# The last stage of an audio tower on one core: GpSimd sums the experts and ends both norms, and every engine gets a new order

## The chip, the cores and the metric

The kernel runs on one core of a Trainium2 chip. The core has five engines with queues of their own: TensorE (matmul, written PE in the profile), VectorE (DVE), ScalarE (ACT), GpSimd (POOL) and SyncE (SP, here the issuer of DMAs). They agree by semaphores. The metric is the device time of one execution in microseconds, and it is compared by medians of several runs.

## The reference, cut to what matters

Five parts run one after the other on 32 batches of 375 tokens with 64 features: token selection, relative attention, experts with top-2 gates, slice attention, and a last part of query experts, the only one touched here. Cut to its steps:

```python
# x: [32, 375, 64]; NH = 4 heads, NE = 4 query experts, d = 16
sx = einsum('bsh,ndh->bnsd', x, hl_w) + hl_b
q, k, v = einsum(sx, wq), einsum(sx, wk), einsum(sx, wv)      # q has NE experts
att = softmax(einsum('bnesd,bntd->bnest', q, k) * d**0.5 + causal)
out = einsum('bnest,bntd->bnesd', att, v); out = where(sx == 0, 0, out)
gs = softmax(einsum(out, gate_w) + gate_b)
mixed = einsum('bnsed,bnse->bnsd', out, gs)                   # sum over the experts
resid = sx[arange(nh), arange(nh)]                            # "the first heads"
hn = layernorm(mixed + resid, ln_g, ln_b)                     # norm 0, over 16 features
hx = where(fx == 0, 0, relu(fx @ fc1.T + b1)); hx = where(fx == 0, 0, hx @ fc2.T + b2)
hx = layernorm(hx + fx, fnorm_g, fnorm_b)                     # norm 1
out = fout * softmax(fout @ fgate_w.T)[..., None]; h = h + out
```

## The kernel before, in words

`query_experts` is a software pipeline over the 32 batches. Every engine has a function `step(r, par)` with the calls of round r in a written order; `bs[i]` is batch r - i, which is i rounds behind the newest one (a lag of i), and `LAGS` is the greatest lag. The helper `rounds` (line 263) writes the first LAGS + 3 rounds out, rounded up so that the rest divides by three, then makes a hardware loop over three rounds a turn, and writes the last LAGS rounds out. With LAGS = 5 that is 8 rounds, 8 turns of the loop and 5 rounds. Nothing but the written orders and the semaphores sets when work happens.

What happens to one batch, with its lag in the kernel before:

- Lag 0: VectorE takes the statistics of the input norm (`start_norm`), GpSimd its root (`take_norm_root`, lines 1253 and 1255), VectorE applies it, and TensorE turns the input and projects queries and keys in three matmuls (`project`, L2201). ScalarE copies each result twice, as bf16 (`first_part`, L2472) and whole (`whole`, L2476). GpSimd then splits it into three bf16 parts: `leave_rest` (L2891) and two instructions of `other_parts` (L2895, L2896), once for each of the three.
- Lag 1: the rest of the splitting, and on SyncE `stack`: it waits for all parts, stores them to DRAM in one DMA (L2157), waits for that, and loads them with 12 DMAs as six stacked groups of rows, into Q (L2161) and K (L2163). TensorE projects the values. `store` writes a finished batch.
- Lag 2: `scores_for_max` in 28 units (L2230, with a mask matmul, L2219), the first of which waits for `stack`. VectorE takes each maximum (L2685).
- Lag 3: `turn_max` on TensorE (L2267), `keep_max` on ScalarE, whose DMA puts the negated maxima into a row of Q. Then `scores_for_exp` in 28 units (L2242, L2219), ScalarE's exponentials (L2495), and `weigh_values` (L2256; e is the expert and jt the column tile, so that 3,2 is the last). ScalarE keeps each expert's context (`keep_context`, L2500), and GpSimd masks it (`mask_context`, L2903).
- Lag 4: the last units of these (exponential scores 24 to 27, values 2,2 and 3,x, context 3 and its mask), `select` and its copies, the gates, and `weigh_experts` (L2659), all on VectorE but for the matmuls and exponentials. Then on VectorE `add_experts` (two instructions of L2663) and `add_first` (one more). Then `centre` and `variance` of norm 0 with the squares on ScalarE, on GpSimd `take_root` (L2911 to L2914: scale, eps, power -1/2, times gamma), on VectorE `finish_mixed` (times the root L2659, plus beta L2663), on TensorE `turn_mixed` (L2285).
- Lag 5: two layers, norm 1 in the same manner (`finish_out` on VectorE), `turn_out` (L2303), the last gate, `hand_out`.

`wait_ge` waits until a semaphore has a value, `own.link` is a wait of an engine for its own instruction. The orders in `step` begin on TensorE with `scores_for_max` 0 and 1, then `turn_max`, `first_layer`, 2, and `weigh_values` 2,2. The last `weigh_values` (3,2) stands behind 9 units for the maximum and 7 for the exponentials. On ScalarE `keep_context` 3 stands behind exponential 3 and `keep_values`.

Of the kernel before, what the change touches and what calls it, by code (L numbers as in the profile page):

```python
# [23 lines left out]
D = 64  # L24
# [2048 lines left out]
def query_experts(k, res, qk_dram, out):  # L2073
# [24 lines left out]
    LAGS = 5  # L2098
    with ExitStack() as ctx:
# [31 lines left out]
        max_stacked = sem("max_stacked")  # L2131
        e_ready, e_done, v_done, c_kept, c_masked = map(sem, ("e", "e_done", "v_done", "c_kept", "c_masked"))
        sel_ready, sel_read, wc_done, g_ready, gex_done, sq_ready, sq_done, vs_ready, root_done = map(
            sem, ("sel", "sel_read", "wc", "g", "gex", "c", "sq", "vs", "root"))
# [13 lines left out]
        def _(sp):  # L2148
# [33 lines left out]
        def _(pe):  # L2182
# [131 lines left out]
            def step(r, par):  # L2314
                on, bs = [alive(r - i, nb) for i in range(LAGS + 1)], [r - i for i in range(LAGS + 1)]
                s = [(par - i) % 3 for i in range(LAGS + 1)]
                if on[2]:
                    scores_for_max(bs[2], s[2], 0)
                    scores_for_max(bs[2], s[2], 1)
                if on[3]:  # L2320
                    turn_max(bs[3], s[3])
                if on[5]:
                    first_layer(bs[5], s[5])
                if on[2]:
                    scores_for_max(bs[2], s[2], 2)
                if on[4]:
                    weigh_values(bs[4], s[4], 2, 2)
                    scores_for_exp(bs[4], s[4], 24)
                    scores_for_exp(bs[4], s[4], 25)
                if on[2]:  # L2330
                    scores_for_max(bs[2], s[2], 3)
                    scores_for_max(bs[2], s[2], 4)
                if on[5]:
                    second_layer(bs[5], s[5])
                if on[2]:
                    scores_for_max(bs[2], s[2], 5)
                if on[4]:
                    scores_for_exp(bs[4], s[4], 26)
                    scores_for_exp(bs[4], s[4], 27)
                    weigh_values(bs[4], s[4], 3, 0)  # L2340
                if on[3]:
                    scores_for_exp(bs[3], s[3], 0)
                if on[1]:
                    project_values(bs[1], s[1])
                if on[2]:
                    scores_for_max(bs[2], s[2], 6)
                if on[4]:
                    weigh_values(bs[4], s[4], 3, 1)
                if on[3]:
                    scores_for_exp(bs[3], s[3], 1)  # L2350
                if on[2]:
                    scores_for_max(bs[2], s[2], 7)
                    scores_for_max(bs[2], s[2], 8)
# [640 lines left out]
```

## Time and profile before

| what | value |
|---|---|
| median of 3 runs | 3435.04 us (3432.09 to 3435.05) |
| profiled execution | 3466.84 us, span 3465.1 us |
| busy, share of the span | PE 90%, DVE 76%, ACT 53%, POOL 37% |
| the last stage | from about 2060 us to the end |
| the costliest line in it | L2685, the maxima on DVE: 896 instructions |

In the profile times are us from the start of the span unless marked ns. A number in brackets behind a row is the idle time of that engine ahead of the instruction, with what ended it. The granted clock (PEclk) is the mean share of TensorE's full speed in that stretch. "issue" is time in which the engine waited for nothing that the profile shows.

### The profile page before, as it was taken

What the parts mean: (1) busy time and instruction counts of PE and PEld (TensorE: products, weight loads), DVE (VectorE), ACT (ScalarE), POOL (GpSimd) and SP (SyncE); (2) the same over time, 40 slices, a digit from 0 to 9 for tenths busy, and PEclk for the clock granted to TensorE, in tenths of its full rate; (3) what the DMA queues carried; (4) which work ended last, traced back from release to release, by engine and by line L of the source; (5) the groups of instructions that cost most, each with busy time, mean ns of one, the idle gap of its engine ahead of it and who ended that gap; (6) DMA issues with size and microseconds to landing.
All of it is one profiled execution on the core that took longest, in us unless ns stands there. A gap on an engine that the chain in (4) does not pass through costs nothing. (4 is left out here: it accounts for less than half of the span.)

```text
span 3465.1 us, 81189 instructions
## 1 busy us (share of the span) xinstructions
PE 3104.9 (90%) x24976; PEld 2206.2 (64%) x24976; DVE 2647.0 (76%) x7766; ACT 1820.8 (53%) x4488; POOL 1289.4 (37%) x1356
## 2 busy tenths in 40 slices
PE   0599999999999799989999956999999999999995
PEld 0488888888888544436777734666666666666663
DVE  4788888888887588866888844788778777877773
ACT  0255555555555455546666612555555555555552
POOL 0344444444444244420000003455445444544432
PEclk9999999999999899997888856899889988988896
DMA  4100000000000000000000005334334333333330
GB/s 136 35 22 16 20 20 14 20 20 14 20 20 2 1 1 0 0 0 1 0 0 0 0 1 80 56 57 71 61 60 66 58 58 58 57 59 67 63 43 4
DMA packets 114142, 111.03 MB, mean 32 GB/s; under 512 B 67960, under 2 KB 105336, under 8 KB 113432
## 3 DMA queue, kind: packets, MB, share of 16 engines
q1 hardware_dynamic: 112792, 106.85, 17.2%
q8 instruction: 137, 2.24, 0.3%
q14 instruction: 189, 1.55, 0.2%
q10 hardware_dynamic: 1024, 0.39, 0.0%
HBM read 76.01 MB, written 30.82 MB: 31 GB/s over the span
## 5 line engine op out<-in xcount | busy, mean ns | idle before, releaser
L2685 DVE TENSOR_REDUCE qe_top<-psum 125x1 f32<-125x375 f32 (+2 forms) x896 | 501.6, 597 | 260.5 <-PE psum L2219 257.1
L2495 ACT ACTIVATE qe_E<-psum 125x375 f32<-125x375 f32 (+1 forms) x896 | 459.7, 531 | 298.7 <-PE psum L2219 281.0
L2219 PE MATMUL psum<-bconst 125*125 125x125 bf16 (+2 forms) x1792 | 494.5, 276 | 0.0
L611 PE MATMUL psum<-Q,K 96*125 96x125 f32 (+3 forms) x2304 | 404.5, 311 | 0.4 <-ACT E L822 0.4
L2230 PE MATMUL psum<-qe_K,qe_Q 96*125 96x375 bf16 (+2 forms) x1536 | 334.5, 301 | 63.1 <-DMA qe_K<-query_key_parts 35.0
L611 PEld LDWEIGHTS psum<-Q,K 96*125 96x125 f32 (+1 forms) x2304 | 334.5, 189 | 24.5 <-issue 1.2
L2242 PE MATMUL psum<-qe_Q,qe_K 97*125 97x375 bf16 (+2 forms) x1536 | 339.7, 301 | 2.4 <-ACT qe_E L2495 2.0
L1161 POOL TENSOR_TENSOR Q<-rot 64x375 f32<-64x375 f32 (+1 forms) x256 | 306.0, 1215 | 73.4 <-DVE rot L962 61.4
L822 ACT ACTIVATE E<-psum 125x500 f32<-125x500 f32 x384 | 226.2, 589 | 169.5 <-PE psum L631 166.3
L2230 PEld LDWEIGHTS psum<-qe_K,qe_Q 96*125 96x125 bf16 x1536 | 182.4, 148 | 174.4 <-DVE qe_top L2685 78.8
L2219 PEld LDWEIGHTS psum<-bconst 125*125 125x125 bf16 x1792 | 268.4, 150 | 9.7 <-issue 6.9
L2242 PEld LDWEIGHTS psum<-qe_Q,qe_K 97*125 97x125 bf16 x1536 | 184.4, 149 | 132.6 <-issue 64.8
L817 ACT CAST half_scores<-psum 125x250 bf16<-125x250 f32 x384 | 141.0, 367 | 221.9 <-PE psum L616 192.3
L2256 PE MATMUL psum<-qe_E,qe_v_aug 125*32 125x375 f32 (+2 forms) x3072 | 253.6, 412 | 0.8 <-ACT qe_E L2495 0.5
L921 DVE SCALAR_TENSOR_TENSOR counted<-s_row,s_loc,bconst 125x750 bf16<-125x750 f32 x192 | 236.4, 1231 | 5.8 <-DMA s_row<-scores 5.3
L2903 POOL TENSOR_TENSOR qe_cT<-qe_cU,qe_nz 128x375 f32<-128x375 f32 x128 | 120.3, 940 | 289.2 <-ACT qe_cU L2500 289.2
L1169 POOL TENSOR_TENSOR x_left<-x_gated,x_three 125x384 f32<-125x384 f32 x32 | 29.3, 917 | 499.1 <-ACT x_three L773 499.1
L992 DVE TENSOR_REDUCE mx<-psum 125x1 f32<-125x250 f32 x384 | 158.8, 414 | 72.4 <-PE psum L624 68.1
L1572 POOL TENSOR_TENSOR x_prob<-fconst,x_shifted 125x24 f32<-125x24 f32 x32 | 133.2, 4162 | 165.2 <-DVE x_shifted L1489 165.2
L1778 ACT ACTIVATE s_E<-psum,s_neg_top 125x64 f32<-125x64 f32 x768 | 168.4, 339 | 6.2 <-DVE s_neg_top L1880 5.5
L2891 POOL TENSOR_TENSOR qe_rest<-qe_rest,qe_parts 128x375 f32<-128x375 f32 x96 | 105.3, 1097 | 175.3 <-ACT qe_rest L2476 175.3
L987 DVE TENSOR_TENSOR most<-psum,half_scores 125x250 bf16<-125x250 f32 x384 | 156.5, 408 | 12.1 <-ACT half_scores L817 10.7
(353 smaller groups left out, 7234.5 us busy)
## 6 DMA issues: line engine op xcount, KB each, us to landing
qe_Q<-query_key_parts SPq DMA_DIRECT2D x192, 187.5 KB, 6.1
query_key_parts<-qe_parts SPq DMA_DIRECT2D x32, 843.8 KB, 3.7
s_row<-scores SPq DMA_DIRECT2D x32, 366.2 KB
qe_K<-query_key_parts SPq DMA_DIRECT2D x192, 46.9 KB, 6.6
x_chunks<-x SPq DMA_DIRECT2D x8, 750.0 KB
x_tokens<-x SPq DMA_DIRECT2D x32, 187.5 KB
out<-qe_hout SPq DMA_DIRECT2D x32, 93.8 KB
weights<-weights_in SPq DMA_DIRECT2D x1, 2395.5 KB, 9.2
```

The source lines that it names most:

```text
L611: nc.tensor.matmul(out[:, first * TP:(first + n) * TP].rearrange("p (o q) -> p o q", o=n), t.K[0:rows(h), par, h, jt * TP:(jt + 1) * TP], ...
L822: nc.scalar.activation(t.E[:, slot(par, u)], bank[0:TP, 5 + u % 3, 0:4 * TP], ACT.Exp, scale=scale).then_inc(e_done, 1)
L921: nc.vector.scalar_tensor_tensor(t.counted[:], t.s_row[:, par, :], t.s_loc[:, c:c + 1], B("tie")[:, c, :], ALU.subtract, ALU.is_ge, accum_ ...
L992: nc.vector.tensor_reduce(t.mx[:, u:u + 1], bank[0:TP, 4, 0:2 * TP], AX, ALU.max).then_inc(max_found, 1)
L1161: last = nc.gpsimd.tensor_tensor(t.Qb(par)[at:at + D, h, part, 0:cols], t.rot[at:at + D, p, 2 * part, 0:cols], t.rot[at:at + D, p, 2 * par ...
L1778: last = nc.scalar.activation(E[:, par, it, h * G:(h + 1) * G], bank[0:TP, 2 + it, h * G:(h + 1) * G], ACT.Exp, bias=neg_top[:, it * HS + ...
L2219: return nc.tensor.matmul(out, B("ident_b")[0:TP, 0:TP], rhs, start=False, stop=True, skip_group_check=True)
L2230: nc.tensor.matmul(out[:, i * cols:(i + 1) * cols], Q[0:RS, slot, h * EE + e, it * TP:(it + 1) * TP], K[0:RS, slot, h, 0:cols], start=i == ...
L2242: nc.tensor.matmul(out[:, i * cols:(i + 1) * cols], K[:, slot, h, jt * TP:(jt + 1) * TP], Q[:, slot, h * EE + e, jt * TP:S], start=i == 0, ...
L2256: last = nc.tensor.matmul(bank[32 * h:32 * h + 32, 0, jt * TP:S], v_aug[:, slot, jt, 32 * h:32 * h + 32], E[:, e % 2, a:a + cols], start=j ...
L2495: nc.scalar.activation(E[:, e % 2, a:a + width], bank[0:TP, 4 + n % 2, 0:width], ACT.Exp).then_inc(e_done, 1)
L2685: nc.vector.tensor_reduce(dst, src, AX, ALU.max).then_inc(m_read, 1)
```

## The change

Four things are changed in `query_experts`, and what is computed stays the same. `add_experts` and `add_first` become one GpSimd function of three additions. `take_root`, `finish_mixed` and `finish_out` become one GpSimd function `finish_norm(b, slot, i)`, which multiplies the rooted gamma by y and adds beta. LAGS is 6, so that 11 rounds are written out ahead of 7 turns of the loop and 6 behind it. And every engine's order is new, with all steps but `start_norm` one lag later.

```diff
-    LAGS = 5
+    LAGS = 6
@@ SyncE
-                if on[1]:
-                    stack(r - 1, (par - 1) % 3)
+                if on[2]:
+                    stack(r - 2, (par - 2) % 3)
@@ VectorE: add_experts, add_first, finish_mixed and finish_out are gone
             def weigh_experts(b, slot):
                 own.wait(dve)
+                wait(dve, y_ready, b)
...
             def centre(b, slot, i):
-                own.wait(dve)
+                if i == 0:
+                    dve.wait_ge(y_ready, b + 1)
+                else:
+                    own.wait(dve)
...
             def variance(b, slot, i):
                 dve.wait_ge(sq_done, 2 * b + i + 1)
-                wait(dve, root_done, 2 * b + i)
+                if i == 0:
+                    wait(dve, fo_ready, b)
+                else:
+                    dve.wait_ge(fx_ready, b + 1)
@@ GpSimd
+            def add_experts(b, slot):
+                pool.wait_ge(wc_done, b + 1)
+                four = wc[:].rearrange("p (t e) f -> p t (e f)", t=NT)
+                own.link(pool, plus(four[:, :, 0:2 * D], four[:, :, 0:2 * D], four[:, :, 2 * D:]))
+                own.link(pool, plus(by_tile(y[:]), four[:, :, 0:D], four[:, :, D:2 * D]))
+                plus(by_tile(y[:]), by_tile(y[:]), res[:]).then_inc(y_ready, 1)
...
+            def finish_norm(b, slot, i):
                 pool.wait_ge(vs_ready, 2 * b + i + 1)
...
-                nc.gpsimd.tensor_tensor(rooted[:], root[:].rearrange("p (a o) -> p a o", o=1).to_broadcast((TP, NT * HE, DH2)),
-                                        gamma[:, i], ALU.mult).then_inc(root_done, 1)
+                own.link(pool, nc.gpsimd.tensor_tensor(rooted[:], wide, gamma[:, i], ALU.mult))
+                own.link(pool, nc.gpsimd.tensor_tensor(rooted[:], rooted[:], y[:], ALU.mult))
+                if i == 0:
+                    wait(pool, fx_turned, b)
+                    wait(pool, sq_ready, 2 * b)
+                    plus(fx[:, :, 0:D], by_tile(rooted[:]), by_tile(beta[:, 0])).then_inc(fx_ready, 1)
+                else:
+                    wait(pool, fo_turned, b)
+                    wait(pool, h_ready, b * 16)
+                    plus(fo[:, :, 0:D], by_tile(rooted[:]), by_tile(beta[:, 1])).then_inc(fo_ready, 1)
@@ GpSimd, step (the whole new order, "if on[i]" left out)
+  mask_context(5, 0) finish_norm(6, 0) mask_context(5, 1) take_norm_root(1)
+  leave_rest(2, 0) mask_context(5, 2) finish_norm(6, 1) mask_context(5, 3)
+  other_parts(2, 0) leave_rest(2, 1) leave_rest(2, 2) other_parts(2, 1) other_parts(2, 2)
+  add_experts(5)
```

In the last hunk the first number is the lag. The order before was: mask_context(4, 0), take_root(5, 0), leave_rest(1, 1), other_parts(1, 0), mask_context(4, 1) and (4, 2), take_root(5, 1), mask_context(4, 3), leave_rest(1, 2), other_parts(1, 1), take_norm_root(0), other_parts(1, 2), leave_rest(0, 0).

TensorE's new order, with M for `scores_for_max` (lag 3) and E for `scores_for_exp`, begins: M0 M1, values 2,2, E22 of lag 5, first_layer, M2, E23, turn_max, E24, M3 M4, E25, second_layer, E26, M5 M6, E27, M7, project_values, values 3,0, M8, E0 of lag 4, M9, E1, values 3,1, M10, E2, values 3,2. It ends: M26, values 2,0, E20 E21, project 2, values 2,1, M27, turn_mixed. On ScalarE a round begins with exponentials 0, 1, 2, then keep_context 3 and keep_values. On VectorE start_norm (lag 0) stands behind maximum 23, apply_norm (lag 1) behind maximum 15, and weigh_experts is followed by maximum 19, divide_out, maximum 20, hand_out and centre 0.

## Rows read from the trace of the kernel before

**Rows 1.** The page, part 1: busy us (share of the span) x instructions.
```profile
PE 3104.9 (90%) x24976; PEld 2206.2 (64%) x24976; DVE 2647.0 (76%) x7766; ACT 1820.8 (53%) x4488; POOL 1289.4 (37%) x1356
```

**Rows 2.** Timeline of TensorE: start us, us, instruction, [idle before it <-releaser].
```profile
2103.75 0.57 PE L2230 MATMUL psum<-qe_K,qe_Q 96*125 96x375 bf16 x1 [9.24 <-DMA qe_K<-query_key_parts]
...
2134.22 0.57 PE L2230 MATMUL psum<-qe_K,qe_Q 96*125 96x375 bf16 x1 [5.66 <-DMA qe_K<-query_key_parts]
...
2480.56 0.37 PE L2230 MATMUL psum<-qe_K,qe_Q 96*125 96x375 bf16 x1 [0.87 <-DMA qe_K<-query_key_parts]
...
2494.31 0.42 PE L2256 MATMUL psum<-qe_E,qe_v_aug 125*32 125x125 f32 x8
...
2521.25 0.37 PE L2230 MATMUL psum<-qe_K,qe_Q 96*125 96x375 bf16 x1 [0.59 <-DMA qe_K<-query_key_parts]
...
2564.67 0.57 PE L2230 MATMUL psum<-qe_K,qe_Q 96*125 96x375 bf16 x1 [3.16 <-issue]
...
2728.21 0.37 PE L2230 MATMUL psum<-qe_K,qe_Q 96*125 96x375 bf16 x1 [0.35 <-DMA qe_K<-query_key_parts]
```

**Rows 3.** Stretches: us, busy us (x) of PE, PEld, DVE, ACT, POOL, PEclk, DMA, GB/s.
```profile
2246.96:3337.44 1090.48, 1026.01 (x8415) 691.77 (x8415) 854.62 (x2014) 604.05 (x1370) 525.66 (x615) 0.90 0.39 62
2282.94:2319.30 36.36, 34.47 (x312) 23.66 (x313) 31.83 (x76) 22.30 (x52) 19.91 (x24) 1.00 0.43 68
2728.21:2764.36 36.15, 34.65 (x312) 23.56 (x313) 31.84 (x77) 22.47 (x52) 20.09 (x24) 1.00 0.42 69
2480.56:2521.25 40.69, 39.22 (x313) 26.18 (x313) 31.55 (x76) 22.52 (x51) 19.61 (x23) 0.87 0.37 61
```

**Rows 4.** Waits of TensorE, 2246 to 3337 us: total us, times, longest.
```profile
PE psum L2230 <- issue: 23.5, 7, 3.7
PE psum L2285 <- DVE qe_fx L2663: 19.5, 27, 0.8
PE psum L2230 <- DMA qe_K<-query_key_parts: 14.3, 17, 1.8
```

**Rows 5.** Timeline of ScalarE: keep_context 3 in the round from 2480.56.
```profile
2495.86 0.49 ACT L2500 COPY qe_cU<-psum 128x375 f32<-128x375 f32 x1
```

**Rows 6.** Timeline of GpSimd and SyncE, round from 2480.56.
```profile
2490.37 0.21 POOL L2911 TENSOR_TENSOR qe_root<-qe_var,fconst 125x12 f32<-125x12 f32 x1 [4.37 <-DVE qe_var L2748]
...
2496.43 0.89 POOL L2903 TENSOR_TENSOR qe_cT<-qe_cU,qe_nz 128x375 f32<-128x375 f32 x1 [2.61 <-ACT qe_cU L2500]
2497.28 1.01 POOL L2891 TENSOR_TENSOR qe_rest<-qe_rest,qe_parts 128x375 f32<-128x375 f32 x1
2498.37 0.85 POOL L2895 TENSOR_TENSOR qe_parts<-qe_rest,qe_zeros 128x375 bf16<-128x375 f32 x1
...
2500.10 0.19 POOL L1253 TENSOR_TENSOR qn_rstd<-qn_mean_var,fconst 125x3 f32<-125x3 f32 x1
...
2501.20 0.84 POOL L2895 TENSOR_TENSOR qe_parts<-qe_rest,qe_zeros 128x375 bf16<-128x375 f32 x1
...
2503.01 0.34 SPq L2157 DMA_DIRECT2D query_key_parts<-qe_parts  x1
```

**Rows 7.** Timeline of GpSimd and SyncE, round from 2728.21.
```profile
2735.11 0.21 POOL L2911 TENSOR_TENSOR qe_root<-qe_var,fconst 125x12 f32<-125x12 f32 x1 [2.77 <-DVE qe_var L2748]
...
2739.53 0.89 POOL L2903 TENSOR_TENSOR qe_cT<-qe_cU,qe_nz 128x375 f32<-128x375 f32 x1 [0.97 <-ACT qe_cU L2500]
...
2746.11 0.34 SPq L2157 DMA_DIRECT2D query_key_parts<-qe_parts  x1
```

**Rows 8.** Groups, 2246 to 3337 us: busy us, mean ns of one | idle before.
```profile
L2663 DVE SCALAR_TENSOR_TENSOR qe_wc<-qe_wc 125x384 f32<-125x384 f32 x27 | 30.1, 1115 | 0.9
L2663 DVE SCALAR_TENSOR_TENSOR qe_fx<-qe_y,qe_beta 125x192 f32<-125x192 f32 x27 | 27.0, 999 | 0.9
...
L2663 DVE SCALAR_TENSOR_TENSOR qe_y<-qe_wc 125x192 f32<-125x192 f32 x27 | 9.7, 358 | 0.9
...
L2914 POOL TENSOR_TENSOR qe_rooted<-qe_root,qe_gamma 125x192 f32<-125x192 f32 x54 | 27.7, 513 | 4.2
```

**Rows 9.** Timeline of SyncE: the second batch's store.
```profile
2116.30 0.34 SPq L2157 DMA_DIRECT2D query_key_parts<-qe_parts  x1
```

More of the change, by code:

```diff
@@ new lines, in step @@
+                if on[4]:
+                    turn_max(bs[4], s[4])
+                if on[5]:
+                    scores_for_exp(bs[5], s[5], 24)
+                if on[3]:
+                    scores_for_max(bs[3], s[3], 3)
+                    scores_for_max(bs[3], s[3], 4)
+                if on[5]:
+                    scores_for_exp(bs[5], s[5], 25)
+                if on[6]:
+                    second_layer(bs[6], s[6])
+                if on[5]:
+                    scores_for_exp(bs[5], s[5], 26)
@@ new lines, in step @@
+                if on[4]:
+                    weigh_values(bs[4], s[4], 1, 2)
+                    scores_for_exp(bs[4], s[4], 16)
+                    scores_for_exp(bs[4], s[4], 17)
+                if on[1]:
+                    project(bs[1], s[1], 1)
+                if on[3]:
+                    scores_for_max(bs[3], s[3], 24)
+                if on[4]:
+                    scores_for_exp(bs[4], s[4], 18)
+                if on[3]:
+                    scores_for_max(bs[3], s[3], 25)
+                if on[4]:
+                    scores_for_exp(bs[4], s[4], 19)
@@ new lines, in step @@
+                if on[3]:
+                    scores_for_max(bs[3], s[3], 26)
+                if on[4]:
+                    weigh_values(bs[4], s[4], 2, 0)
+                    scores_for_exp(bs[4], s[4], 20)
+                    scores_for_exp(bs[4], s[4], 21)
+                if on[1]:
+                    project(bs[1], s[1], 2)
+                if on[4]:
+                    weigh_values(bs[4], s[4], 2, 1)
+                if on[3]:
+                    scores_for_max(bs[3], s[3], 27)
+                if on[5]:
+                    turn_mixed(bs[5], s[5])
@@ L2767, in add_layers @@
                 own.up(plus(by_tile(y[:]), by_tile(y[:]), fx[:, :, 0:D]))
-            def finish_out(b, slot):
-                dve.wait_ge(root_done, 2 * b + 2)
-                wait(dve, fo_turned, b)
-                own.link(dve, times(y[:], y[:], rooted[:]))
-                plus(fo[:, :, 0:D], by_tile(y[:]), by_tile(beta[:, 1])).then_inc(fo_ready, 1)
             def less_max(b, slot):
@@ new lines, in step @@
+                if on[5]:
+                    gate_weights(bs[5], s[5])
+                    expert_weights(bs[5], s[5])
+                    weigh_experts(bs[5], s[5])
+                if on[3]:
+                    maximum(bs[3], s[3], 19)
+                if on[6]:
+                    divide_out(bs[6], s[6])
+                if on[3]:
+                    maximum(bs[3], s[3], 20)
+                if on[6]:
+                    hand_out(bs[6], s[6])
+                if on[5]:
+                    centre(bs[5], s[5], 0)
```

574 lines of the change are left out of this document (255 added, 319 removed).

## The prediction

> **What bounds the kernel now.** I read the page's engine totals first [rows 1]: TensorE is busy for 90% of the span, VectorE for 76%, GpSimd for 37%. The change touches only the last stage, so I read that stage by rounds. A round is one pass of each engine's written order. It begins on TensorE where the first scores_for_max waits for the stacked queries and keys, and those starts are in [rows 2]. From 2246.96 to 3337.44 us there are 27 such rounds with nearly full load: 1090.48 us, 40.39 us each [rows 3]. The same row has VectorE at 854.62 us, which is 31.7 a round, and GpSimd at 19.5. Neither is close to the round, so taking work from VectorE is worth nothing by itself.
>
> The rounds come in three kinds [rows 3]. Where the granted clock is 1.00 (2.4 GHz throughout), a round is 36.15 to 36.36 us with TensorE busy for 34.5. Where it is 0.87, part of the round runs at 1.2 GHz: 40.69 us with 39.2 busy. Once in three rounds there is the loop's turn, 3.16 us of "issue" before the first matmul: from 2521.25 to 2564.67, 43.42 us [rows 2]. The slow stretch lies at the start of a round: the same matmul takes 0.57 us at 2564.67 and 0.37 at 2728.21 [rows 2].
>
> Each round starts behind a short wait. Over the 27 rounds TensorE waits 14.3 us for the keys' DMA (17 times) and 23.5 us for the loop's turn (7 times) [rows 4]. So a second bound, a cycle, is in step with TensorE. It runs from the round's start through the last weigh_values (its 3,2), ACT's keep_context 3 and GpSimd's mask_context 3 to the splitting of the next batch's parts. Then come SP's store of the parts and its 12 loads, and the next round's start. In the round from 2480.56 its stations are: weigh_values at 2494.31, mask_context 3 at 2496.43, store at 2503.01, next start at 2521.25 [rows 2, 6]. In offsets that is 13.75, 15.87, 22.45 and 40.69 us. From store to start it is 18.24 us. In the full-clock round it is 2728.21, 2739.53, 2746.11, 2764.36 [rows 2, 3, 7]: offsets 11.32, 17.90, 36.15, and again 18.25 from store to start. A change to the time from round start to parts done therefore appears one to one in the round, unless TensorE is slower still.
>
> **The change, part by part.** (a) VectorE gives up seven instructions a round: the wide sum of experts of 1.115 us, its second half of 0.358, the first heads, two products with the root, and two sums with beta, the first of 0.999 [rows 8]. The four without a row are between 0.358 and 1, so 3.9 to 6.5 us; I take 5.5, nearer the long ones, since most of them run beside GpSimd. It waited for TensorE or GpSimd elsewhere anyway, so the direct gain is 0. VectorE is not late at the round's start.
>
> (b) GpSimd takes them. No row has them there. By the nearest rows an operation of 192 columns is 0.51 us (the product with gamma [rows 8]) and one of 375 columns 0.89 to 1.01 (mask and leave_rest [rows 6]). That gives 0.95 + 5 x 0.51 = 3.5 us a round, 23 of 40 busy. The bounds are 2.5 us, if they ran at VectorE's uncontended 0.358, and 6, if each stretched as VectorE's sums do. Three of them (add_experts) stand after the parts and delay nothing in the cycle. Two stand in finish_norm 1, ahead of mask_context 3, which is where they can hurt.
>
> The row for that stretching: VectorE's sum into fx has mean 0.999 us where another sum of the same shape has 0.358 [rows 8], and the long ones run while GpSimd is busy. The Trainium skill (GPSIMD Engine Reference, section 1, Specifications) has GpSimd share its SBUF interfaces with VectorE, in contention with VectorE instructions that read two SBUF inputs. Section 4.1, Engine selection, of the same page sends two-input elementwise work to VectorE, about twice as fast. The row gives 0.51 against 0.358, a factor of 1.4. By the page's factor finish_norm would be 0.4 us longer. In (e) that makes a full-clock round 39.0 and leaves the slow-start round and the forecast as they are.
>
> (c) When does mask_context 3 start? It needs GpSimd free of finish_norm 1 and keep_context 3 done. Two more units of scores_for_exp (22, 23) and two of scores_for_max (9, 10) now precede the last weigh_values on TensorE. At full clock a unit of 375 columns costs 0.22 us by the spacing of starts, so 0.9 us, and up to 0.8 more if two of them run at 1.2 GHz. Against that, keep_context 3 now stands right behind exponential 2, while before it stood behind exponential 3 and keep_values: weigh_values was over at 2494.73 and the copy began at 2495.86 [rows 2, 5], 1.1 us that go. Finish_norm 1 begins behind variance 1, at offset 6.90 in the full-clock round and 9.81 in the other [rows 6, 7], plus some 0.4 to 0.7 for the moved units. It takes the root as before, 3.4 us (from 2735.11 until VectorE took over, with the 0.51 of the product in it), and two more of 0.51 with their waits, 4.7 us. So it ends at about 12.2 and 15.3. At full clock the norm decides, and the mask starts at 12.2 rather than 11.32: +0.9. With the slow start keep_context decides, at 15.9: +0.1.
>
> (d) What GpSimd does between mask_context 3 and the store. Before, that was mask, leave_rest 2, parts 1, norm root, parts 2: 2496.43 to 2503.01, 6.58 us [rows 6]. After, the order is mask, parts 0, leave_rest 1 and 2, parts 1, parts 2. It gains a leave_rest (1.0) and a pair of parts (2498.37 to 2500.10, 1.7) and loses the norm root (2500.10 to 2501.20, 1.1): +1.6 us, 8.15. The 12 loads behind it are unchanged, 18.25.
>
> (e) So the cycle is 12.2 + 8.15 + 18.25 = 38.6 us at full clock (before 36.15), and 15.9 + 8.15 + 18.25 = 42.3 with the slow start (before 40.69). TensorE's own work stays at 34.5 or 39.2, so it would stand 3 to 4 us at each start. Which clock? All ten round starts of the 27 that stand behind a wait of 1.3 us or more have the slow stretch (2564.67 is one [rows 2]), and of the other 17 eight have not. I take the slow one always: 42.3. In rounds with the loop's turn TensorE has 39.4 + 3.3 = 42.7, so the turn is nearly hidden, +0.4 six times. Sum: 27 x (42.3 - 40.39) = +52, +3 for the turns, +55.
>
> (f) Lags 6 instead of 5: one round more, which holds only start_norm of the first batch, about 1 us. In the fill the new order helps. Before, the second batch's parts waited behind the norm root of the third, which waited for VectorE's maxima: second store at 2116.30, starts at 2103.75 and 2134.22 [rows 2, 9]. Now the second store can follow the first stacking at once, at 2104, and the next start comes at VectorE's pace (28 maxima of 0.6 us and norms, 20 us) or the DMA's (18.3): 10 us earlier. Of the next rounds one gains about 3 and one loses as much. Fill: -10 + 1 = -9. The drain's chain keeps its steps; GpSimd's are longer and hand-overs fewer: 0.
>
> (g) Waits added: y_ready on VectorE ahead of centre 0. Behind it stand variance and the last maxima. GpSimd needs about 2.2 us from wc_done, during which VectorE has a maximum, divide_out, another maximum and hand_out, 2.5 us. Cost 0; without that cover 2 us a round, off the path until TensorE's turn_mixed. That step gets fx 2 us ahead of its place, so the 0.7 us it waits now (19.5 us in all, 27 times [rows 4]) goes, but only into the DMA's wait. turn_max is later by 1.5 us. Its row's DMA lands in 2 us and exponential scores 0 come 3 us after: nothing. ACT's first_part 0 waits for the store, which comes 1.6 us later, and so does project 0 by its place: nothing.
>
> Total: +55 - 9 = +46 us. The profiled execution is 3466.84 us (span 3465.1) and would become 3513. The median of the runs is 3435.04, 31.8 less. I carry the difference over and forecast 3481.
>
> **Rivals.** A, faster: the clock does not fall although TensorE waits. Then each round is 38.6, 27 x (38.6 - 40.39) = -48, with the fill -57: 3378. If half of the rounds keep it: 27 x (40.45 - 40.39) = +2, with the fill -7: about 3430. For it: eight rounds keep the full clock, and the new order packs TensorE more evenly behind the wait. Against it: ten of ten after the longer waits.
>
> The Trainium skill (TensorE: Matmul & The Clock Gate, Part 1, What's actually happening) has a clock that falls after idling and returns after steady work. The starts of [rows 2] agree that it falls after the longer waits, but the round from 2480.56 has it (clock 0.87 [rows 3]) behind 0.87 us of waiting.
>
> B, no change: steps of the cycle were counted as serial which are not, for instance GpSimd gets mask_context 3 and the parts 1.6 us earlier than I say. Then the cycle equals the old one, and only the fill is won: 3435 - 9 + 5 = 3431. C, much slower: GpSimd's operations stretch beside VectorE's, as VectorE's do beside GpSimd (0.999 against 0.358 [rows 8]), or finish_norm 1 decides in both clocks. 1.5 us more a round, 27 x 1.5 = 41: 3522. D, the change does what it is named for and VectorE's relief shortens the round: spoken against by [rows 3], where VectorE has 9 us a round to spare.
>
> **Numbers.** Forecast 0.55, C 0.14, A in full 0.10, A in half of the rounds 0.10, B 0.09, D 0.02. What a measurement of this kernel can tell from no change is 0.2%, 7 us. Faster: A 0.14, B 0.05, D 0.02, 0.21. Same: 0.08. Slower: 0.71. The likeliest alone has 3455 to 3515; with the others the range is 3390 to 3530.
>
> **What would show it.** Right: TensorE's wait for the keys' DMA at the round's start grows from 0.5 a round to about 3. From mask_context 3 to the store it is 8.1 us, the rounds are near 42.3, the clock is near 0.86 in each, and VectorE's busy time falls by 5 us a round with no gain. Wrong: a wait under 1 us at the starts, or rounds of 36 to 38 us at clock 1.00.

## The result and the profile after

| | before | changed |
|---|---|---|
| median of the runs (lowest to highest), us | 3435.05 (3432.09 to 3446.91) | 3535.08 (3530.95 to 3537.27) |
| ratio to before, 95% interval | | 1.0288 (1.0251 to 1.0325) |
| profiled run, us; its granted clock | 3466.84; 0.907 | 3536.61; 0.895 |

The change costs 2.9%, 100 us. The forecast was 3481 (+46), and the highest value of its range 3530: the sign and the cycle through the DMA came out, the size did not.

The page's engine totals, answering to [rows 1], and then TensorE's main wait over 26 rounds (line waited for, releaser: total us, times, longest), answering to [rows 4]:

```profile
PE 3132.3 (89%) x24976; PEld 2246.6 (64%) x24976; DVE 2498.9 (71%) x7542; ACT 1823.0 (52%) x4488; POOL 1411.8 (40%) x1580
```
```profile
PE psum L2230 <- DMA qe_K<-query_key_parts: 78.1, 20, 5.0
```

VectorE has 148 us less to do, and the time is longer. The wait for the keys' DMA was 14.3 us over 27 rounds [rows 4]; it is 78.1 over 20 of these 26. At the six others the wait is put down to the loop's turn (31.7 us together; before 23.5 in seven). Stretches of the changed kernel, with the columns of [rows 3]; the first holds 26 rounds, the next two one each, and the last two cut up the start of the round from 2662.52:

```profile
2271.15:3405.42 1134.27, 1022.27 (x8104) 708.67 (x8104) 700.04 (x1749) 584.97 (x1319) 605.32 (x775) 0.86 0.36 57
2662.52:2705.67 43.15, 39.67 (x313) 27.37 (x313) 27.09 (x68) 22.62 (x51) 23.53 (x30) 0.86 0.37 59
2880.25:2925.23 44.98, 39.77 (x312) 27.72 (x313) 26.93 (x68) 22.69 (x51) 23.38 (x30) 0.84 0.35 55
...
2662.52:2672.52 10.00, 10.00 (x49) 6.97 (x50) 4.49 (x10) 3.59 (x8) 0.00 (x0) 0.50 0.02 6
2672.52:2675.02 2.50, 2.50 (x16) 2.03 (x15) 2.10 (x5) 1.12 (x3) 2.05 (x4) 0.56 0.00 0
```

A round is 1134.27 / 26 = 43.63 us (before 40.39), VectorE is busy for 26.9 of it (before 31.7), and each of the 26 rounds shows a clock of 0.84 to 0.92, while before eight of 27 kept full clock. In the round from 2662.52 TensorE runs at 1.2 GHz (0.50) for the first 10 us and most of the next 2.5. TensorE at the round starts (start, us, instruction, [idle before it <-releaser]), answering to [rows 2], and the last weigh_values of the middle round:

```profile
2617.91 0.57 PE L2230 MATMUL psum<-qe_K,qe_Q 96*125 96x375 bf16 x1 [4.30 <-DMA qe_K<-query_key_parts]
2662.52 0.57 PE L2230 MATMUL psum<-qe_K,qe_Q 96*125 96x375 bf16 x1 [5.08 <-issue]
2705.67 0.57 PE L2230 MATMUL psum<-qe_K,qe_Q 96*125 96x375 bf16 x1 [3.32 <-DMA qe_K<-query_key_parts]
```
```profile
2678.58 0.42 PE L2256 MATMUL psum<-qe_E,qe_v_aug 125*32 125x125 f32 x8
```

Then ScalarE's keep_context 3, GpSimd from finish_norm 1 to the last part, and SyncE's store in that round, answering to [rows 5 to 7]:

```profile
2679.16 0.47 ACT L2506 COPY qe_cU<-psum 128x375 f32<-128x375 f32 x1
```
```profile
2673.62 0.21 POOL L2906 TENSOR_TENSOR qe_root<-qe_var,fconst 125x12 f32<-125x12 f32 x1
...
2677.89 0.59 POOL L2893 TENSOR_TENSOR qe_fo<-qe_rooted,qe_beta 125x192 f32<-125x192 f32 x1 [0.16 <-POOL qe_rooted L2910]
2679.71 0.98 POOL L2887 TENSOR_TENSOR qe_cT<-qe_cU,qe_nz 128x375 f32<-128x375 f32 x1 [1.23 <-ACT qe_cU L2506]
...
2682.52 1.75 POOL L2875 TENSOR_TENSOR qe_rest<-qe_rest,qe_parts 128x375 f32<-128x375 f32 x2
...
2687.06 0.85 POOL L2880 TENSOR_TENSOR qe_parts<-qe_rest,qe_parts 128x375 bf16<-128x375 f32 x1
```
```profile
2687.93 0.34 SPq L2157 DMA_DIRECT2D query_key_parts<-qe_parts  x1
```

So the cycle can be read off: start 2662.52, mask_context 3 at 2679.71 (offset 17.19), store at 2687.93 (8.22 later), next start 2705.67 (17.74 later). The norm ended at 2678.48 and GpSimd stood 1.23 us for ScalarE's copy: here the norm on GpSimd doesn't set the start of the mask, the time at which TensorE reaches weigh_values does. So it is in 24 of the 26 rounds; in the two with the highest clock (from 2401.34 and 2749.57) the mask follows the norm's last sum directly, at 15.14. Means over the rounds with all three stations, split by what ends the wait (before, three more rounds ended with a wait for VectorE):

| mean us | rounds | length | start to mask_context 3 | mask to store | store to next start |
|---|---|---|---|---|---|
| before, ended by the DMA | 19 | 40.04 | 15.09 | 6.55 | 18.41 |
| before, loop's turn | 7 | 41.13 | 13.42 | 6.71 | 21.00 |
| changed, ended by the DMA | 22 | 43.36 | 16.85 | 8.16 | 18.35 |
| changed, loop's turn | 6 | 44.62 | 16.79 | 8.10 | 19.73 |
| before, 27 rounds from 2246.96 | 27 | 40.39 | 14.74 | 6.59 | 19.07 |
| changed, 27 rounds from 2227.42 | 27 | 43.63 | 16.83 | 8.15 | 18.66 |

So GpSimd's longer splitting behind the mask is 1.56 us of the 3.24 a round has grown by. The mask itself starts 2.09 us later, with four more units of scores ahead of weigh_values and the lower clock at the round's start, and 0.41 us comes back between store and start.

GpSimd's new operations, by group over the 26 rounds (busy us, mean ns of one | idle before), answering to [rows 8]:

```profile
L2893 POOL TENSOR_TENSOR qe_wc<-qe_wc 125x384 f32<-125x384 f32 x26 | 26.0, 998 | 107.1 <-DVE qe_wc L2666 107.1
L2910 POOL TENSOR_TENSOR qe_rooted<-qe_rooted,qe_y 125x192 f32<-125x192 f32 x52 | 30.8, 592 | 4.1
```

There are six of 192 columns a round at 0.59 us and one of 384 at 1.00: 4.55 us.

### The profile page after: what moved, and what is told of

The parts are those of the page before. It is cut to its first block and busy times, and to the rows that moved or that the text cites. A ratio compares the mean times of both kernels' runs of the same rounds, so it can differ in the third digit from the quotient of the medians.

```text
span 3534.8 us, 80669 instructions
## 1 busy us (share of the span) xinstructions
PE 3132.3 (89%) x24976; PEld 2246.6 (64%) x24976; DVE 2498.9 (71%) x7542; ACT 1823.0 (52%) x4488; POOL 1411.8 (40%) x1580
## 5 line engine op out<-in xcount | busy, mean ns | idle before, releaser
L2219 PE MATMUL psum<-bconst 125*125 125x125 bf16 (+2 forms) x1792 | 512.9, 286 | 0.0
L2230 PE MATMUL psum<-qe_K,qe_Q 96*125 96x375 bf16 (+2 forms) x1536 | 355.6, 313 | 132.7 <-DMA qe_K<-query_key_parts 100.4
L2230 PEld LDWEIGHTS psum<-qe_K,qe_Q 96*125 96x125 bf16 x1536 | 196.1, 156 | 264.8 <-issue 180.6
L2242 PE MATMUL psum<-qe_Q,qe_K 97*125 97x375 bf16 (+2 forms) x1536 | 359.8, 311 | 2.6 <-ACT qe_E L2501 2.5
L2219 PEld LDWEIGHTS psum<-bconst 125*125 125x125 bf16 x1792 | 282.0, 157 | 13.8 <-issue 10.8
L2242 PEld LDWEIGHTS psum<-qe_Q,qe_K 97*125 97x125 bf16 x1536 | 196.0, 154 | 120.5 <-issue 69.8
L2256 PE MATMUL psum<-qe_E,qe_v_aug 125*32 125x375 f32 (+2 forms) x3072 | 245.0, 401 | 0.6 <-ACT qe_cU L2506 0.6
```

The source lines that it names most:

```text
L2219: return nc.tensor.matmul(out, B("ident_b")[0:TP, 0:TP], rhs, start=False, stop=True, skip_group_check=True)
L2230: nc.tensor.matmul(out[:, i * cols:(i + 1) * cols], Q[0:RS, slot, h * EE + e, it * TP:(it + 1) * TP], K[0:RS, slot, h, 0:cols], start=i == ...
L2242: nc.tensor.matmul(out[:, i * cols:(i + 1) * cols], K[:, slot, h, jt * TP:(jt + 1) * TP], Q[:, slot, h * EE + e, jt * TP:S], start=i == 0, ...
L2256: last = nc.tensor.matmul(bank[32 * h:32 * h + 32, 0, jt * TP:S], v_aug[:, slot, jt, 32 * h:32 * h + 32], E[:, e % 2, a:a + cols], start=j ...
```

## The experiments

Three theories. **Cycle**: a round lasts from its start to the end of the splitting and on through store and loads; what GpSimd does between mask_context 3 and the store is paid in full. **Sums**: the sums and norms on GpSimd are what costs. **Order**: TensorE's and ScalarE's new order is slower by itself. In the diffs the guards and arguments are shortened. Each ratio is to the kernel before as it ran beside that experiment; its median there was 3435.95 to 3458.22 us, so times of two experiments that differ by 20 us are better compared by their ratios.

**GpSimd's order alone, in the kernel before.** leave_rest 1 and the first pair of other_parts go behind mask_context 3, as in the changed kernel; nothing else differs from before.

```diff
                 take_root(.., 0)
-                leave_rest(.., 1)
-                other_parts(.., 0)
...
                 mask_context(.., 3)
+                leave_rest(.., 1)
+                other_parts(.., 0)
                 leave_rest(.., 2)
```

> The kernel before (old orders of TensorE, ScalarE and VectorE, LAGS 5, sums on VectorE) with GpSimd's splitting moved the other way: leave_rest 1 and other_parts 0 of lag 1 stand behind mask_context 3, as in the changed kernel. Theory 1 (the cycle): 6.6 us from the mask to the store become 9.3, every wait at a round's start is over 2 us, the clock falls in each, rounds of 43.5 to 44.5, so 27 x 3.5 = 90 us more than before's 3448, 3520 to 3550: the order of GpSimd alone makes the loss. Theory 3 (TensorE's new order costs the time): 3448 plus at most the 2.7 us of GpSimd off its path, within 15.

Measured: 3529.07 us (3523.25 to 3538.25), ratio 1.0258 (1.0189 to 1.0327). That is 87 us over before's median there (3441.84), inside the range expected (3520 to 3550); but the rounds were not: 42.40 us from store to store, where 43.5 to 44.5 were expected. From mask to store it was 9.45 us. TensorE's waits from 2300 to 3200 us, and one round:

```profile
PE psum L1271 <- DVE qn_xn L1263: 30.2, 21, 1.5
PE psum L2230 <- DMA qe_K<-query_key_parts: 23.7, 15, 2.2
```
```profile
2540.62:2582.35 41.73, 36.12 (x312) 23.89 (x313) 31.12 (x75) 22.44 (x51) 19.64 (x23) 0.94 0.36 60
```

The first wait was not foreseen: take_norm_root stands behind the splitting, so the next batch's norm comes later and TensorE stands at its transposes, 1.4 us a round. But it stands there right behind the store (2551.87 mask, 2561.48 store, 2561.56 transposes), inside the stretch that the loads decide: in 20 of 27 rounds the next start waits for the keys, and these last 15.09 + 9.44 + 18.06 = 42.59 us, the cycle without this wait. So with before's sums and before's orders on the other engines, this one move makes 2.02 of the 3.27 us that the changed kernel loses a batch, from profile to profile (42.40 and 43.65 against 40.38). The rest is ahead of the mask, which starts at 14.21 on the mean of 27 rounds here and at 16.83 in the changed kernel. That the medians lie closer (+87 and +100) is because the changed kernel gains 19.5 us in the fill, which this one doesn't.

**The reverse: the splitting ahead of the masks, in both kernels.** In the changed kernel all of leave_rest and other_parts goes ahead of mask_context 2 (new_parts_early); in the kernel before, leave_rest 2 and the last two pairs (old_parts_early).

```diff
                 leave_rest(.., 0)
+                other_parts(.., 0)
+                leave_rest(.., 1)
+                leave_rest(.., 2)
+                other_parts(.., 1)
+                other_parts(.., 2)
                 mask_context(.., 2)
                 finish_norm(.., 1)
                 mask_context(.., 3)
-                other_parts(.., 0)
...
-                other_parts(.., 2)
 # old_parts_early
                 mask_context(.., 1)
+                leave_rest(.., 2)
+                other_parts(.., 1)
+                other_parts(.., 2)
                 mask_context(.., 2)
```

> The changed kernel with one edit: in GpSimd's order the five calls that split the next batch's parts stand right behind leave_rest 0, ahead of mask_context 2, instead of behind mask_context 3. Theory 1 (the cycle from the round's start over mask_context 3, the parts and the stacking to the next start): the store goes out some 9 us after the round's start (when the last scores for the exponentials have freed the slot) instead of 25, TensorE's 3 to 5 us of waiting for the keys vanish, rounds fall from 43.8 to 36 to 39.5, the time from 3535 to about 3385 (3340 to 3425). Theory 2 (the sums on GpSimd cost the time by their length or by contention with VectorE): the sums are all still there, so 3535 within 15. Theory 3 (the new order of TensorE is what is slow): also about 3535.

> The kernel before with the same edit alone: leave_rest 2 and other_parts 1 and 2 of lag 1 stand ahead of mask_context 2. Theory 1: the old kernel hung on the same cycle; without it only TensorE is left, 39.2 us a round where its clock falls and 35 where it does not. At least the 14.3 us of waits for the keys go (3421); with the clock kept up in most rounds about 3350. Theories 2 and 3 see nothing to gain in it: 3435 within 7.

Measured: new_parts_early 3414.00 (3401.46 to 3428.78), 0.9913 (0.9885 to 0.9941); old_parts_early 3383.28 (3381.34 to 3384.73), 0.9815 (0.9761 to 0.9868). The first lies in the range that **Cycle** expected (3340 to 3425), the second between its two values (3421 and 3350), and neither kernel has a wait of TensorE for the keys' DMA any more. One station was forecast wrongly: in new_parts_early the store goes out 20.6 us after the round's start on the mean, not 9, for GpSimd stands for VectorE in add_experts and the first norm and comes to the splitting only then. What is late next in the changed kernel, TensorE's waits of new_parts_early from 2300 to 3200 us:

```profile
PE psum L2303 <- POOL qe_fo L2893: 43.6, 17, 2.8
PE psum L2230 <- issue: 18.4, 6, 3.2
```

The move takes 121 us from the changed kernel. It now waits 2.6 us, 17 times, for the attention's norm, which the splitting delays. Whether the change's other parts are slower than before by themselves, this kernel can't tell; the series on the splitting below does.

**Sums and orders apart.** old_order_gpsimd_sums is the kernel before with weigh_experts' sums and both norms' ends on GpSimd (finish_norm, add_experts); new_order_vector_sums is the changed kernel with these back on VectorE, in the new order.

```diff
 # old_order_gpsimd_sums, GpSimd's order
-                take_root(.., 0)
+                finish_norm(.., 0)
...
+                add_experts(..)
 # new_order_vector_sums, VectorE's order
                 weigh_experts(..)
+                add_experts(..)
+                add_first(..)
...
+                finish_out(..)     # behind maximum 10
...
+                finish_mixed(..)   # behind maximum 25
```

> One part of the change alone: the three additions and both norm endings on GpSimd, with LAGS 5 and every order as before (add_experts at the end of GpSimd's round). Theory 1: finish_norm 1 is over 15 us after a round's start, just ahead of mask_context 3 at 15.9, nothing is added behind the mask, so 3435 to 3455. Theory 2: most of the 100 us, 3500 to 3535.

> The other part alone: LAGS 6 and the new orders, with the additions and norm endings on VectorE (behind weigh_experts, behind maximum 10 and behind maximum 25, as they stood before) and only the roots on GpSimd. Theory 1: GpSimd's work between mask_context 3 and the store is the same 8.1 us, and the mask waits for keep_context 3, so 3520 to 3540. Theory 2: back to 3435 to 3450.

Measured: old_order_gpsimd_sums 3461.58 (3442.01 to 3469.17), 1.0033 (0.9998 to 1.0068), which can't be told from no change, a little above the 3435 to 3455 expected; new_order_vector_sums 3536.48 (3503.30 to 3541.85), 1.0236 (1.0158 to 1.0315). The loss goes with the orders, not with the sums: as its cause **Sums** falls. In the second the stations are those of the changed kernel: start to mask 16.69, mask to store 8.17, store to start 18.28.

**The norm's place.** new_vector_parts_early joins the sums on VectorE with the early splitting; new_early_norm_first is new_parts_early with finish_norm 1 ahead of mask_context 2.

```diff
 # new_vector_parts_early: new_order_vector_sums with
 # the move of new_parts_early
 # new_early_norm_first
+                finish_norm(.., 1)
                 mask_context(.., 2)
-                finish_norm(.., 1)
                 mask_context(.., 3)
```

> The new orders with the sums on VectorE and the splitting ahead of mask_context 2. With the sums on GpSimd and the same early splitting, 3414 us, TensorE stood 43.6 us in 17 waits for the end of norm 1 (turn_out). If that is the price of ending the norm on GpSimd, the waits go and the time falls by 17 x 2.5 us and the clock that comes back with them: 3340 to 3375. If the new orders themselves hold TensorE there, it stays within 10 of 3414.

> The changed kernel with the early splitting (3414 us) and finish_norm 1 ahead of mask_context 2 too. If the mask and the splitting ahead of the norm hold turn_out, its waits of 2.6 us fall by 0.9 at least and the time by 15 to 40 us (3375 to 3400). If variance 1 is simply late for the place that turn_out has in TensorE's order, less than 10 us.

Measured: new_early_norm_first 3389.82 (3388.47 to 3397.32), 0.9843 (0.9780 to 0.9907), as expected (3375 to 3400), its wait for qe_fo down from 43.6 to 27.8 us. new_vector_parts_early 3443.42 (3437.42 to 3462.02), 1.0012 (0.9984 to 1.0040): a miss. TensorE's first row of waits there, 2300 to 3200 us:

```profile
PE psum L2230 <- DVE qe_top L2692: 40.7, 16, 2.6
```

finish_out behind maximum 10 makes VectorE wait for GpSimd's root (over both norms 49.9 us in 39 waits), and the maxima behind it wait as well. So this kernel measures the place I gave finish_out, not the price of the sums; the last experiment repeats it with another place.

**The DMA's share of the cycle.** new_four_loads is the changed kernel with four of the six groups loaded and the rest of Q and K zeroed once. It leaves out a third of the loads, and its scores lack two groups; it serves for the time alone. Nothing on GpSimd differs.

```diff
-    for g, (qp, kp) in enumerate(zip(q_parts, k_parts)):
+    for g, (qp, kp) in enumerate(zip(q_parts[:4], k_parts[:4])):
```

> The changed kernel with four of the six stacked groups of queries and keys loaded (8 DMAs of 12 a round; the rows of the other two are set to zero once, so the scores lack them). Nothing on the engines changes but the issues on SyncE. Theory 1: the time from the store to the next start falls from 18.3 us by a third of the loads' 14.4, to 13.5 to 14.5; so rounds are 39.5 to 40, with the waits at the starts at 1 us or less, and TensorE the bound where the clock falls. Total 3535 - 28 x 4 + some 10 us once for the zeroing: about 3430. Theories 2 and 3: rounds stay at 43.8.

Measured in a single run: 3361.22 us, clock 0.926. Store to next start is 14.3 us on the mean of the 23 rounds without a turn, instead of 18.35; from mask to store it is still 8.15. Three rounds with one turn:

```profile
2480.59:2592.27 111.68, 106.50 (x936) 74.26 (x937) 81.70 (x204) 66.87 (x153) 70.14 (x90) 0.95 0.30 54
```

That is 37.2 a round; over all batches it is 36.83, and the six rounds ahead of the first turn take 34.24 each, all with the changed kernel's order on every engine. TensorE's and ScalarE's new order is therefore not slow by itself: **Order** falls. The forecast had the direction and not the size (39.5 to 40 a round, 3430 in all): it put TensorE at the low clock, and in 17 of 27 rounds the clock was 1.00. In those six rounds the mask starts at 12.05, as GpSimd's norm ends (12.09); step (c) of the prediction had 12.2 for full clock. Shortening the cycle at its DMA end does what shortening it at its GpSimd end does.

**How much of the splitting behind the mask?** Both start from the changed kernel. new_half_parts_early leaves leave_rest 2 and two pairs behind mask_context 3, new_last_parts_late only the last pair; new_last_parts_norm_first is the latter with finish_norm 1 first.

```diff
 # new_last_parts_late
                 leave_rest(.., 0)
+                other_parts(.., 0)
+                leave_rest(.., 1)
+                leave_rest(.., 2)
+                other_parts(.., 1)
                 mask_context(.., 2)
                 finish_norm(.., 1)
                 mask_context(.., 3)
-                other_parts(.., 0)
...
-                other_parts(.., 1)
                 other_parts(.., 2)
 # new_half_parts_early: of these, ahead of mask_context 2 only
+                other_parts(.., 0)
+                leave_rest(.., 1)
 # new_last_parts_norm_first, against new_last_parts_late
+                finish_norm(.., 1)
                 mask_context(.., 2)
-                finish_norm(.., 1)
```

> The changed kernel with other_parts 0 and leave_rest 1 ahead of mask_context 2, about where the kernel before had them; leave_rest 2 and other_parts 1 and 2 stay behind mask_context 3. A dose between: from mask to store 5.5 us. Theory 1: the cycle is 12.2 + 5.5 + 18.3 = 36.0 us at full clock and 17.1 + 5.5 + 18.3 = 40.9 with a slow start, against 43.8 now: waits of 1.6 to 1.9 us, nearly all starts slow, about 3535 - 28 x 2.8 = 3457 (3420 to 3470).

> The changed kernel with all of the splitting but the last other_parts ahead of mask_context 2; other_parts 2 alone stays behind mask_context 3. Theory 1: from the mask to the store 2.7 us instead of 8.15, so the keys land 12.2 + 2.7 + 18.3 = 33.2 us after a full-clock start and 38.1 after a slow one, both inside TensorE's 34.4 and 39. GpSimd is free again when variance 1 is done, so turn_out no longer waits 2.6 us as in the version with all of it early (3414). Rounds of 34.4 as with four loads, the total 3340 to 3365, below both kernels. If instead any splitting ahead of the norm costs, it stays at 3400 to 3415.

> As the version with only other_parts 2 behind mask_context 3, and finish_norm 1 ahead of mask_context 2. If the norm's end is what TensorE's turn_out waits for even there, 5 to 15 us faster than it; if that wait is gone already, the same within 5 us, or up to 10 slower where mask_context 2 and 3 then hold select 0 (it did that 14 times for 3.7 us in the version with all parts early).

Measured: 3403.24 (3398.70 to 3407.55), 0.9851 (0.9795 to 0.9907); 3324.00 (3319.86 to 3325.30), 0.9615 (0.9562 to 0.9669); 3333.27 (3326.12 to 3342.51), 0.9655 (0.9599 to 0.9711). The first two came out faster than their ranges (3420 to 3470 and 3340 to 3365), the third in its last case. In order of the time from mask to store, with the mean interval between the stores of the 5th and the 32nd batch (turns included) in the profiled run:

| kernel | mask to store | per batch | clock | median |
|---|---|---|---|---|
| changed | 8.16 | 43.65 | 0.895 | 3535.08 |
| new_half_parts_early | 5.40 | 38.88 | 0.917 | 3403.24 |
| new_last_parts_late | 2.67 | 36.51 | 0.933 | 3324.00 |

The first 2.76 us are worth 4.77 a batch, the next 2.73 only 2.37, where TensorE is the bound again. More than one for one, because a shorter wait at the start also goes with a clock that stays up: 0.97 or more in none of the changed kernel's 27 rounds, in 12 of new_half_parts_early's and in 21 of new_last_parts_late's. new_last_parts_late beats both kernels. Three of its rounds, and TensorE's waits from 2300 to 3200 us:

```profile
2459.23:2571.57 112.34, 106.96 (x937) 74.27 (x937) 79.20 (x204) 67.91 (x153) 70.59 (x92) 0.95 0.42 67
```
```profile
PE psum L2230 <- issue: 17.8, 6, 3.2
PE psum L2303 <- POOL qe_fo L2893: 13.5, 17, 0.9
PE psum L2230 <- DMA qe_K<-query_key_parts: 1.8, 2, 1.2
```

TensorE is busy for 107.0 of 112.3 us, and the largest wait left is the loop's turn. The last pair is better behind the mask: each wait for the norm is then 1.8 us shorter (17 of them, 13.5 us in all against 43.6 in new_parts_early), and the keys still land in time but for two rounds. With the norm first its wait shrinks further, to 2.6 us in all, and TensorE stands 4.1 us for the contexts' masks instead. The median is 9 us longer; the two profiled runs differ by only 0.8 us (3326.12 and 3325.30), so the traces don't show where these 9 us arise, only that nothing is won.

**What the sums are worth without the DMA's wait.** new_vector_last_late is new_last_parts_late with the sums and the norms' ends on VectorE, finish_out behind maximum 13.

```diff
 # against new_vector_parts_early, VectorE's order
-                finish_out(..)     # behind maximum 10
...
+                finish_out(..)     # behind maximum 13
```

> The version of 3324 us (new orders, only other_parts 2 behind mask_context 3) with the sums and norm endings back on VectorE; finish_out now stands behind maximum 13 instead of 10, so that it doesn't hold the maxima 2.6 us for the root as in the version of 3443. With the keys' DMA off the path this is the price or gain of the part that gave the change its name. If GpSimd's sums pay, because VectorE is late for TensorE without them: 3340 to 3380. If they cost, because norm 1 ends later on GpSimd (turn_out waits 0.8 us a round there): 3300 to 3320. If neither matters: 3324 within 7.

Measured: 3394.98 (3389.19 to 3396.21), 0.9892 (0.9858 to 0.9927); 38.71 us a batch in the profile against 36.51 with the sums on GpSimd. Its first wait of TensorE from 2300 to 3200 us:

```profile
PE psum L2303 <- DVE qe_fo L2670: 37.0, 23, 1.7
```

So this kernel is 71 us slower than the one with the sums on GpSimd. That is not yet the price of the sums, for again the place of finish_out is in it. In most rounds GpSimd's rooted gamma is ready 1.53 us before VectorE, behind maximum 13, comes to finish_out, and TensorE waits for the result:

```profile
2529.38 0.51 POOL L2922 TENSOR_TENSOR qe_rooted<-qe_root,qe_gamma 125x192 f32<-125x192 f32 x1
...
2531.42 0.35 DVE L2666 SCALAR_TENSOR_TENSOR qe_y<-qe_y,qe_rooted 125x192 f32<-125x192 f32 x1
...
2531.80 0.89 DVE L2670 SCALAR_TENSOR_TENSOR qe_fo<-qe_y,qe_beta 125x192 f32<-125x192 f32 x1
...
2532.74 0.33 PE L2303 MATMUL psum<-fconst,qe_fo 125*128 125x125 f32 x1 [1.58 <-DVE qe_fo L2670]
```

By an estimate from these rows, 27 x 1.53 = 41 of the 71 us can be this place. Behind maximum 10 VectorE waited for the root, behind 13 TensorE waits for VectorE; a place between was not run, so what the sums on GpSimd are worth here stays open. In the changed kernel they were worth nothing (3535.08 against 3536.48), because TensorE was waiting for the keys either way, and in the old order nothing that can be told from no change (1.0033).

The Trainium skill (GPSIMD Engine Reference, section 4.1, Engine selection) would keep elementwise sums on VectorE, with GpSimd about twice as slow on two inputs. The rows agree on the direction for a single instruction, 0.59 us against VectorE's 0.358 at its shortest [rows 8], a factor of 1.65. In the kernel's time the longer instructions did not show: GpSimd is busy for 23.3 of 43.6 us in a round of the changed kernel, and moving the sums left the time as it was in both pairs that keep every order (1.0033; 3535.08 against 3536.48). VectorE's own sums took 1.0 us in some places and 0.36 in others [rows 8], so one factor doesn't describe the two engines here.

## Why the prediction was right in sign and wrong in size

Right: (a), relief for VectorE alone brings nothing; (d), mask to store forecast 8.15, measured 8.16; store to start forecast 18.25, measured 18.35; the clock falls in every round; the norm on GpSimd is not late (4.9 us, forecast 4.7, and in 24 of 26 rounds its end lay ahead of ScalarE's copy); the waits of (g) don't appear among TensorE's. Rival D and rival B are out: VectorE has 4.8 us a round less and TensorE waits longer, and the cycle was serial as counted. TensorE stood 4.2 us at a start (109.8 us over 26), not about 3. Rival C named the right total (3522) by a wrong mechanism. Step (b) counted five operations of 192 columns where there are six, and they took 0.59 us rather than 0.51: 4.55 us a round against 3.5, but not on the cycle. Rival A happened in none of the 26 rounds.

Wrong, from profile to profile, +69.8 us where the sum in (e) and (f) had +46:

| term | forecast | measured |
|---|---|---|
| 27 intervals from the 5th to the 32nd store | +55 | 1178.4 - 1090.1 = +88.3 |
| fill, until the 5th store | -9 | 2209.13 - 2228.62 = -19.5 |
| the rest | 0 | +1.0 |

**Step (c) fails by its size.** I took the slow-start round from 2480.56 and put the mask at 15.9. Behind the longer waits of the changed kernel the slow stretch at the round's start is longer: by the clock, 2 x (1 - 0.86) x 43.63 = 12.2 us on the mean of the 26 rounds, against 2 x 0.13 x 40.69 = 10.6 in the round from 2480.56 [rows 3]. Here are the first 14 us of before's round from 2480.56, the changed round from 2575.05 and the one from 2662.52 (columns of [rows 3]):

```profile
2480.56:2494.56 14.00, 14.00 (x91) 8.88 (x91) 6.86 (x16) 5.02 (x11) 4.20 (x5) 0.63 0.01 3
```
```profile
2575.05:2589.05 14.00, 14.00 (x87) 9.66 (x87) 7.50 (x16) 5.28 (x12) 3.95 (x5) 0.63 0.01 3
2662.52:2676.52 14.00, 14.00 (x75) 9.72 (x76) 6.63 (x15) 4.74 (x10) 3.49 (x4) 0.57 0.02 6
```

Four of the 26 changed rounds have 0.63 there like the round that I took, and in these the mask starts at 15.83 to 15.96: the count of TensorE's work ahead of weigh_values was right. Twenty have 0.51 to 0.58, TensorE's work ahead of weigh_values takes longer by that, and the mean start of the mask is 16.85: 27 x 0.95 = 26 us of the missing 33. The speed of the first matmul alone doesn't tell them apart: it is 0.57 in the three starts above, but 0.37 to 0.39 in eight of the 26, two of which have the mask at 17.42. The kernel before had a round of this kind, from 2887.92, with its mask at 17.13. The forecast had TensorE wait 3 to 4 us at each start and should have taken its stations from a start behind a wait of that kind.

**Step (e), the turns.** I took them as nearly hidden, +0.4 and 42.7 us a round; measured are 44.62. They lie partly behind the DMA's landing: 19.73 against 18.35 from store to start, 1.4 us six times, about 6 us more than forecast. In the turn at 2662.52 the last load of keys was issued at 2652.04, and the slowest of the six took 8.7 us to land: if that was the last, the keys were there at 2660.7, and the first matmul came 1.8 us later. Which part of the turn runs behind the wait, the rows don't show.

**Step (f)** had the fill's sign and half its size; the second store came at 2104.46, where it was forecast, 11.8 us earlier than before [rows 9]. By the third it was 19.9 us (2129.32 against 2149.19), and this was kept; the forecast had let the next rounds even out.

**The median.** I carried over the 31.8 us between before's profiled run and its median. These 31.8 us go with the clock: beside the first experiments the 19 runs of the kernel before go from 3424.56 us at 0.919 to 3470.32 at 0.907. That some of its round starts fall to the low clock in one run and not in the next fits this, but is argued: only one run of it has a trace, and the three behind the median have no clock on record. The changed kernel waits at every start, has the slow stretch in every round, and has nothing of this left to win: clock 0.895 or 0.896 in its runs, 3536.61 in the profile against a median of 3535.08. So 30 us of the +100 are this difference, which the changed kernel lost. Together: 46 + 24 (size of the terms) + 30 (carried over) = 100. This was the largest single error, and it was avoidable: the forecast said itself that all rounds would have the low clock.

Open are two things: why the slow stretch is longer in one round than in another behind waits of nearly the same length (mask at 17.42 behind 3.76 us in the round from 2486.44, at 15.87 behind 3.65 us in the one from 2271.15), and what the sums on GpSimd are worth once the cycle is short.

## What to carry to other kernels

In a pipelined loop that goes through a DMA and back, follow the cycle from the round's start to the next start, and give each instruction in front of the store its full price: here one engine's order, with the same work, spans 3324 to 3535 us. While such a cycle is longer than the busiest engine's work, taking work from another engine changes nothing (3535.08 against 3536.48 us here), so shorten the cycle first and then judge the relief. And find a good place in the new order for each engine's version before comparing who should do a piece of work: here the place of finish_out clouded that comparison twice. Where the time before already scatters with the clock, forecast from the rounds of the kind that the change will leave, and don't carry over a difference between one run and the median that the change takes away.

## What the runs showed of the hardware

Starts behind middling waits are not all alike. In new_half_parts_early, TensorE at two starts and the stretches of the rounds behind them:

```profile
2927.07 0.37 PE L2230 MATMUL psum<-qe_K,qe_Q 96*125 96x375 bf16 x1 [1.52 <-DMA qe_K<-query_key_parts]
...
3005.74 0.37 PE L2230 MATMUL psum<-qe_K,qe_Q 96*125 96x375 bf16 x1 [1.51 <-DMA qe_K<-query_key_parts]
```
```profile
3005.74:3040.46 34.72, 33.89 (x313) 23.73 (x313) 26.59 (x68) 22.42 (x51) 22.60 (x30) 1.00 0.42 71
...
2927.07:2964.12 37.05, 33.87 (x312) 23.70 (x313) 26.80 (x68) 22.45 (x51) 24.99 (x33) 1.00 0.42 67
```

Both keep 2.4 GHz behind a wait of 1.5 us, while in the kernel before the round from 2480.56 fell behind 0.87 [rows 2, 3]. The forecast's "ten of ten" from 1.3 us up described one trace and is no rule. The Trainium skill (TensorE: Matmul & The Clock Gate, Part 1, What's actually happening) lets the clock fall after idling and return after steady work; neither trace contradicts that, but the rule alone doesn't tell these starts apart.

A GpSimd sum of 192 columns with two plain inputs took 0.59 us, the product whose root is spread over the columns 0.51. The turn of the hardware loop costs TensorE about 3 us (17.8 us in six turns of new_last_parts_late), and every trace here shows it as idle time of TensorE (17.4 to 31.7 us in six or seven turns).
